# A state-space mixer and a mixture of experts on one core: the mixer's first half rebuilt by channel

## The chip, the cores and the metric

The kernel runs on one core of one Trainium2 chip. The metric is device time in microseconds (us), the median of several executions. The engines are TensorE (PE; its weight loads are listed as PEld), VectorE (DVE), ScalarE (ACT), GpSimd (POOL) and SyncE (SP), which issues most transfers; ScalarE and GpSimd can issue transfers too.

## The reference, cut to what matters

The input is 8 batches of 512 steps with 128 features, all in float32.

```python
xz = einsum('bld,ed->bel', hidden, W_in); x, z = split(xz)     # 256 channels each
x = silu(causal_conv(x, conv_w, 4 taps per channel) + conv_b)
dtA = exp(log_dt)[:, None] * (-exp(log_A_real) + 1j * A_imag)  # 256 channels x 8 states
Ct = (C_re + 1j * C_im) * (exp(dtA) - 1) / A
k = 2 * real(einsum('hn,hnl->hl', Ct, exp(dtA[:, :, None] * arange(512))))
y = causal_convolution(x, k) + x * D                           # along the 512 steps
y = y * silu(z)
x1 = layernorm(hidden + einsum('bhl,dh->bld', y, W_out))
e = argmax(x1 @ gate_w.T + gate_b + expert_bias)               # one of 8 experts per token
out = layernorm(x1 + relu(x1 @ w1[e] + b1[e]) @ w2[e] + b2[e])
```

## The kernel before, in words

The 4096 tokens are cut into 32 chunks of 128 steps (4 per batch). The long convolution is computed in chunks: inside a chunk by a Toeplitz matrix of the first 128 kernel values, across chunks through the 8 complex states of each channel, for up to three chunks back. The 256 channels form 32 groups of 8.

**Projection (0 to 80 us).** `project` (line 1292) takes 16 steps of two chunks. For each chunk it multiplies the input by four weight matrices `Wx`, one per tap, each already scaled by that tap's weight per channel (line 873), so the four-tap convolution happens inside TensorE's accumulation; `project_gates` (line 1275) adds the product for z. VectorE adds the bias and stores x with the channel in the free dimension (`bias`, line 881), ScalarE stores z (`keep_z`, line 643). Beside this the two engines build the tables: `Ctab`, the powers of the states at steps 0 to 128, as an exponential times a sine with amplitude and phase (arctangent, square root), and `Btab` with `decay`, the same powers counted backwards for three lags, from rows that are sent to DRAM and broadcast. Line 1337 sums the states into kernel rows, which are stored to DRAM (line 414).

**Groups (80 to 130 us).** For each of 32 groups SP loads 512 KB of Toeplitz matrices from DRAM (`load_toeplitz`, line 424, a ring of 8). GpSimd forms the group's state table (`group_tables`, line 515). TensorE multiplies chunks by Toeplitz matrices (`convolve`, line 1370), sums states over three lags (`sum_states`, line 1357), transposes the first product back and adds the states' part (`finish`, lines 1380 and 1384). VectorE masks the states (`states`, line 1044) and multiplies the output by the gates (`output`, line 1057). ScalarE copies and applies Silu in between (lines 713 to 738).

**Quads (130 to 175 us).** Eight quads of four chunks, one batch each. TensorE transposes the gated output (`transpose_gated`, line 1418), ScalarE copies it (line 761), TensorE projects it with the output weights, the residual and the gate logits in one accumulation (lines 1433 and 1435). ScalarE sums squares (line 772), VectorE takes the reciprocal (line 1085), chooses the expert, normalizes (line 1122) and, with counts from TensorE (lines 1449 and 1451), finds each token's row. GpSimd then dispatches the rows: `dispatch` (line 568) sends 128 rows at a time to DRAM by an indirect transfer, each behind a small fill (`apart`, line 558). In the first 52 us SP has written empty rows over the whole buffer of slots (line 409, four transfers of 1.8 to 2.3 MB).

**Blocks (from 173 us).** 39 blocks of 128 rows, each for one expert. SP loads a block's rows (line 450, a ring of 12) and the expert's first weights (line 371, a ring of 4). TensorE transposes and multiplies (lines 1469, 1477, 1487), VectorE adds and normalizes, GpSimd stores each block by an indirect transfer (`store`, line 576), the first 24 behind a small fill. A slot of the row ring is loaded again only when the block twelve before it is stored.

The order on every engine is written out by hand. GpSimd's queue holds the group tables, then the constants of the counting, then all dispatches, then all stores. SP's holds the loads in the order of use.

## Time and profile before

| | us |
|---|---|
| device time, median of 3 runs | 269.08 (268.27 to 269.29) |
| span of the profiled execution, first to last instruction | 263.8 |
| the runs' median over that span | 5.3 |
| TensorE busy | 239.2 (91%) |
| ScalarE busy | 187.1 (71%) |
| VectorE busy | 177.0 (67%) |
| GpSimd busy | 139.8 (53%) |
| moved by DMA | 52.06 MB, 197 GB/s on the average |

The profiled execution's device time is known only through its span; the median less the span, 5.3 us, is what lies around it. Busy times are those of the whole span; the stages differ much. Columns of the groups below are named where they first occur.

### The profile page before, as it was taken

How to read it: one execution, taken by the hardware profiler on the slowest of the kernel's cores; microseconds unless marked ns; L12 is line 12 of the kernel's file. 1: busy time of each engine (PE TensorE's matmuls, PEld its weight loads, DVE VectorE, ACT ScalarE, POOL GpSimd, SP SyncE). 2: the span in 40 equal slices, each digit the busy share in tenths (PEclk: the TensorE clock that was granted, in tenths of full speed). 3: DMA queues.
4: the chain of work that ended last, by engine and by line, in shares of the span. 5: the costliest groups of instructions: out<-in, count | busy, mean ns of one | idle time of the engine just before them, and what ended most of it. 6: DMA issues, size and time to landing. Idle time of an engine off the chain costs nothing.

```text
span 263.8 us, 8892 instructions
## 1 busy us (share of the span) xinstructions
PE 239.2 (91%) x2763; PEld 215.1 (82%) x2764; DVE 177.0 (67%) x552; ACT 187.1 (71%) x528; POOL 139.8 (53%) x208
## 2 busy tenths in 40 slices
PE   8999979999999899999979999359989999999970
PEld 4888768888887678888869999349979999899960
DVE  1889995997218657777724878842877676566672
ACT  2999999856998778888655665207667777667740
POOL 6000000400009989999624687878746656657545
PEclk9999999999999999999999999759999999999995
DMA  7697884600399999999293221647865676677600
GB/s 232 180 313 288 346 334 150 244 0 0 105 310 332 310 279 296 308 320 302 66 361 120 93 93 41 212 92 191 220 179 172 200 210 164 203 195 208 189 34 6
DMA packets 54267, 52.06 MB, mean 197 GB/s; under 512 B 4415, under 2 KB 42817, under 8 KB 54114
## 3 DMA queue, kind: packets, MB, share of 16 engines
q1 hardware_dynamic: 51506, 46.65, 59.2%
q0 software_dynamic: 2304, 4.34, 4.6%
q10 hardware_dynamic: 432, 0.79, 0.8%
q8 instruction: 11, 0.18, 0.3%
q14 instruction: 14, 0.11, 0.1%
HBM read 38.14 MB, written 14.07 MB: 198 GB/s over the span
## 4 chain that ended last, share of the span: by engine, by line
PE 59%; DVE 10%; ACT 10%; POOL 9%; issue 6%; DMA 5%; SPq 1%; DVEq 0%; ACTq 0%; POOLq 0%
PE banks L1292 13%; PE banks L1477 9%; PE banks L1487 8%; PE banks L1370 7%; POOL dispatched_rows L568 5%; ACT BR L672 5%; PE banks L1380 5%; PE banks L1384 4%; PE banks L1275 3%; PE banks L1357 3%; PE banks L1435 2%; DMA X<-dispatched_rows 2%; POOL RE L558 1%; DMA out<-X 1%; POOL out L576 1%
## 5 line engine op out<-in xcount | busy, mean ns | idle before, releaser
L515 POOL TENSOR_TENSOR Wx<-BR,RE 128x384 f32 (+1 forms) x32 | 47.9, 1548 | 27.9 <-PE banks L1292 26.6
L1292 PE MATMUL banks<-Wx,XT 128*128 128x256 f32 x256 | 59.9, 380 | 1.7 <-ACT Z L643 1.7
L809 ACT ACTIVATE Z<-banks,BR 128x128 f32<-128x128 f32 x156 | 44.6, 368 | 18.4 <-PE banks L1477 18.3
L1292 PEld LDWEIGHTS banks<-Wx,XT 128*128 128x128 f32 x256 | 48.4, 190 | 9.0 <-issue 2.2
L576 POOL DMA_INDIRECT out<-X x39 | 38.4, 986 | 27.8 <-DVE X L1233 15.3
L1477 PE MATMUL banks<-Z 128*128 128x128 f32 x312 | 42.7, 281 | 0.4 <-ACT Z L798 0.2
L1487 PE MATMUL banks<-BR,Z 128*128 x312 | 41.1, 276 | 1.2 <-DVE X L1216 1.2
L1477 PEld LDWEIGHTS banks<-Z 128*128 128x128 f32 x312 | 39.0, 196 | 1.0 <-issue 0.5
L1487 PEld LDWEIGHTS banks<-BR,Z 128*128 128x128 f32 x312 | 37.8, 192 | 1.5 <-issue 1.5
L568 POOL DMA_INDIRECT dispatched_rows<-TR,CR x32 | 31.0, 970 | 9.3 <-POOL RE L558 9.3
L1057 DVE TENSOR_TENSOR X<-banks,Z 128x256 f32 (+1 forms) x32 | 20.4, 636 | 9.1 <-PE banks L1384 9.1
L521 POOL MEMSET RE<- 128x128 f32 x1 | 0.2, 205 | 44.0 <-DVE CR L989 44.0
L1370 PE MATMUL banks<-TR,RE 128*32 128x128 f32 x512 | 21.3, 279 | 1.4 <-issue 1.2
L1216 DVE TENSOR_TENSOR X<-banks,X 128x128 f32<-128x128 f32 x39 | 11.3, 289 | 14.9 <-PE banks L1487 13.4
L881 DVE TENSOR_TENSOR X<-banks,cbias 128x512 f32<-128x512 f32 x15 | 15.3, 1062 | 8.5 <-PE banks L1275 8.4
L1435 PE MATMUL banks<-Wx,RE 128*128 128x136 f32 x128 | 20.1, 279 | 0.0
L1370 PEld LDWEIGHTS banks<-TR,RE 128*32 128x32 f32 x512 | 12.3, 109 | 9.4 <-ACT RE L713 5.8
L798 ACT ACTIVATE Z<-banks 128x128 f32<-128x128 f32 x39 | 11.3, 289 | 10.8 <-PE banks L1469 10.3
L1275 PE MATMUL banks<-Win,XT 128*128 128x256 f32 x64 | 18.5, 381 | 0.0
L772 ACT ACTIVATE RE<-banks 128x128 f32<-128x128 f32 x32 | 8.9, 278 | 13.2 <-PE banks L1435 8.8
L558 POOL MEMSET RE<- 128x128 f32 x56 | 12.7, 226 | 9.1 <-DVE CR L1141 7.9
L1044 DVE SCALAR_TENSOR_TENSOR Win<-banks,RE,mask 128x192 f32<-128x192 f32 x32 | 13.4, 418 | 6.1 <-PE banks L1357 4.3
(220 smaller groups left out, 469.6 us busy)
## 6 DMA issues: line engine op xcount, KB each, us to landing
TR<-kernel_rows SPq DMA_DIRECT2D x32, 512.0 KB, 6.5
Z<-w SPq DMA_DIRECT2D x39, 256.0 KB, 3.1
dispatched_rows<-TR SPq DMA_DIRECT2D x3, 2310.0 KB, 8.8
X<-dispatched_rows SPq DMA_DIRECT2D x39, 66.0 KB, 2.1
XT<-hidden_t SPq DMA_DIRECT2D x10, 256.0 KB, 3.1
RE<-decay_and_turns SPq DMA_DIRECT2D x2, 1024.0 KB, 7.4
BR<-w SPq DMA_DIRECT2D x1, 2048.0 KB, 8.2
dispatched_rows<-TR SPq DMA_DIRECT2D x1, 1848.0 KB, 7.8
```

Source lines behind the costliest of these rows:

```text
L515: nc.gpsimd.tensor_tensor(BC[:, k, 0:LAGS, :].rearrange("p m (s r n) -> p (m s) r n", s=STRIPS, r=2), Btab[:, :, :, :, :, one].rearrange(" ...
L558: nc.gpsimd.memset(pause[:, 0:columns], 0.0).then_inc(s_pause, 1)
L568: pool.indirect_dma_start(slots_dram, bass.IndirectOffsetOnAxis(pos[:, batch, k:k + 1], 0), X1[:, batch, k, :], None).then_inc(s_sc[batch] ...
L576: pool.indirect_dma_start(out_rows, bass.IndirectOffsetOnAxis(XS[:, n % ROWS_RING, TOKEN_COL:TOKEN_COL + 1].bitcast(U32), 0), F[:, slot, : ...
L809: last = nc.scalar.activation(HT[:, j, c * P:c * P + P], bank[UP_BANKS[j]][:, c * P:c * P + P], ACT.Relu, bias=B1[:, bass.ds(experts[j] * ...
L1057: tt(group, bank[4 + k][:, 0:GH * TILES].rearrange("p (h t) -> p h t", h=GH), gates, ALU.mult).then_inc(s_yc, 1)
L1275: return mm(bank[Z_BANKS[k]][:, j * CHAN:(j + 1) * CHAN], XT[:, slot, at:at + CHUNK], Win[:, CHAN:], start=True, stop=True)
L1292: last = mm(bank[X_BANKS[k]][:, j * CHAN:(j + 1) * CHAN], XT[:, slot, at:at + CHUNK], Wx[:, tap, :], start=(tap == 0), stop=(tap == TAPS - 1))
L1370: last = mm(yt[part:part + TILES, at:at + P], xg[:, h, :], Tring[:, k, h, :], start=True, stop=True)
L1435: last = mm(projected(slot, k), GT[:, slot, k, j * P:j * P + P], Wo[:, j, :], start=False, stop=(j == 1))
L1477: last = mm(bank[UP_BANKS[m % 4]][:, c * P:c * P + P], WS[:, stage, c * P:c * P + P], XsT[:, m % DEEP, :], start=True, stop=True)
L1487: last = mm(bank[DOWN_BANKS[m % 2]][:, 0:P], HT[:, m % DEEP, c * P:c * P + P], W2[:, e, c * DM:(c + 1) * DM].rearrange("p e d -> p (e d)") ...
```

## The change

The mixer is rebuilt with the channel in the partitions. `project_x` and `project_gates` are now one multiplication each over 512 steps for 128 channels (16 units of x and 16 of gates: 2 channel halves by 8 batches). The taps are added outside TensorE: ScalarE takes the last tap and the bias (`last_tap`), VectorE adds the other three from PSUM (`add_taps`). `turn_x` transposes each unit back, `keep_x` stores it with Silu, `keep_z` stores the gates with Silu.

The tables are rebuilt too. One table of powers `Etab` replaces `Ctab`, `Btab` and `decay`. Sines and cosines are taken at 28 angles only (16 fine, 8 coarse, 3 lags, one half step); GpSimd expands them to 128 steps by products of coarse and fine powers (`expand_half`, two halves of 16 groups), after it has formed the states' weights. `products`, the scratch of that expansion, lies in the upper half of X, and ScalarE waits for the second half of the powers (`s_e1`) before it stores unit 8 there. TensorE transposes the powers (`turn_powers`), sums local states per four groups (`sum_local`), turns them over three lags by matrices `Rot` that GpSimd forms (`turning`, `turn_states`), and adds them to the output by two multiplications of 64 rows each (`add_states`).

The kernel rows are summed and stored in two halves; SP loads five groups' Toeplitz matrices behind the first half and the others behind the second; the ring has 5 places instead of 8. Each group's output is copied (`keep_y`) into a ring of 4 and returned by one GpSimd transfer (`send_y`) of 128 KB into Y, where the channel lies in the partitions, four partitions per group. After the last transfer Y is multiplied by the gates per quad, quads 1, 3 and 5 by GpSimd, the others by VectorE (`gate`). TensorE's transpositions in the quads and ScalarE's copies of them go. All eight batches of the input stay in SBUF. The rows that no token takes are no longer emptied over the whole buffer: SP writes 128 empty rows behind each expert's last row, eight small transfers ahead of blocks 8 to 11.

The core of the diff:

```diff
+        def expand(engine, out, part, by_coarse, by_fine):
+            count = part.stop - part.start
+            shape = [P, count, COARSE, FINE]
+            return engine.tensor_tensor(
+                out.rearrange("p g (b a) -> p g b a", b=COARSE), by_coarse[:, part, :].unsqueeze(3).to_broadcast(shape),
+                by_fine[:, part, 0:FINE].unsqueeze(2).to_broadcast(shape), ALU.mult)
...
+            store_rows(0)
+            for g in range(T_SLOTS):
+                load_toeplitz(g)
+            store_rows(1)
+            for g in range(T_SLOTS, GROUPS):
+                load_toeplitz(g)
...
+            def expand_half(part, ready):
+                expand(nc.gpsimd, Etab[:, part, :], part, first_coarse, cosine)
+                done(expand(nc.gpsimd, products[:, part, :], part, second_coarse, sine))
+                tt(Etab[:, part, :], Etab[:, part, :], products[:, part, :], ALU.add).then_inc(ready, 1)
+
+            def send_y(g):
+                pool.wait_ge(s_yt, g + 1)
+                home = bass.AP(Y[:, :, :, :].tensor, g * 2 * TOKENS, [[GROUPS * 2 * TOKENS, 4], [2 * P, TILES], [1, 2 * P]])
+                pool.dma_start(home, YT[:, g % Y_RING, :]).then_inc(s_yd[g % Y_RING], 16)
+
+            pool.wait_ge(s_far, 1)
+            expand_half(slice(0, HALF), s_e0)
+            turning(slice(0, HALF))
+            expand_half(slice(HALF, GROUPS), s_e1)
...
+            for n in POOL_QUADS:
+                gate(nc.gpsimd, n).then_inc(s_gp, 1)
             nc.gpsimd.memset(OH[:, :, :, 4], 0.0)
             nc.gpsimd.memset(carry, 1.0).then_inc(s_oc, 1)
...
+            act.wait_ge(s_e1, 1)
+            keep_x(8)
+            last_tap(10)
+            for n in range(TURNS):
+                keep_y(4 * n)
+                if n + 1 < TURNS:
+                    keep_local(n + 1)
+                if n == 0:
+                    keep_rows(1)
+                    keep_powers(4)
...
+            def add_taps(u):
+                j = u // BATCH
+                dve.wait_ge(s_x3, u + 1)
+                for back in range(1, TAPS):
+                    if back > 1:
+                        dve.wait_ge(s_xk, u * LAGS + back - 1)
+                    stt(xc[:, u % 2, back:], bank[u % 2][:, 0:SEQ - back], channel[:, j, TAPS - 1 - back:TAPS - back],
+                        xc[:, u % 2, back:], ALU.mult, ALU.add).then_inc(s_xk, 1)
...
+            def add_states(g):
+                halves = output_banks(g)
+                pe.wait_ge(s_v, g + 1)
+                for j in range(2):
+                    rows = slice(j * 64, (j + 1) * 64)
+                    last = mm(halves[j][:, 0:P], V[rows, g % V_RING, :, :].rearrange("p h t -> p (h t)"), Etab[rows, g, :],
+                              start=False, stop=True)
+                last.then_inc(s_y, 1)
```

## Rows read from the trace of the kernel before

**Rows 1.** Busy time by stage: stretch, length, busy us (instructions), clock, DMA share, GB/s.

```profile
0.00:80.00 80.00, 77.02 (x394) 64.97 (x395) 58.01 (x111) 67.42 (x111) 8.40 (x37) 1.00 0.62 210
80.00:130.00 50.00, 48.53 (x1414) 39.66 (x1414) 34.83 (x66) 41.11 (x113) 47.50 (x34) 1.00 1.00 285
130.00:175.40 45.40, 36.04 (x294) 34.74 (x293) 30.35 (x143) 22.41 (x90) 28.64 (x57) 0.93 0.43 143
175.40:264.00 88.60, 77.64 (x663) 75.77 (x663) 53.80 (x234) 56.16 (x215) 55.24 (x82) 0.94 0.59 165
```

**Rows 2.** The chain of waits: start us, us, what.

```profile
36.37 0.43 PE banks L1275 x2
...
64.86 1.96 PE banks L1337 x64
...
81.90 0.57 PE banks L1370 x16
...
142.88 0.88 PE banks L1418 x8
...
148.76 0.96 POOL dispatched_rows L568
```

**Rows 3.** GpSimd in order of time: start us, us, engine, line, operation.

```profile
141.19 0.20 POOL L558 MEMSET RE<- 128x128 f32 x1 [7.10 <-DVE CR L1141]
...
188.43 0.96 POOL L568 DMA_INDIRECT dispatched_rows<-TR,CR  x1 [0.28 <-POOL RE L558]
...
190.42 1.00 POOL L576 DMA_INDIRECT out<-X  x1 [0.81 <-POOL RE L558]
...
261.07 0.98 POOL L576 DMA_INDIRECT out<-X  x1 [0.30 <-issue]
```

**Rows 4.** ScalarE in order of time, the start.

```profile
3.89 1.28 ACT L619 ACT_TABLE_LOAD   x1 [3.74 <-DMA RE<-states]
...
5.32 0.21 ACT L620 ACTIVATE RE<-RE 128x32 f32<-128x32 f32 x1
```

**Rows 5.** Groups of instructions on VectorE: busy us, mean ns of one, idle before.

```profile
L1122 DVE TENSOR_TENSOR TR<-banks,rs 128x512 f32<-128x512 f32 x8 | 5.3, 665 | 0.0
...
L983 DVE TENSOR_TENSOR BR<-BR 128x2064 f32<-128x2064 f32 x2 | 4.6, 2310 | 0.1
```

**Rows 6.** Groups of instructions on ScalarE.

```profile
L662 ACT ACTIVATE RE<-RE,tau 128x2048 f32<-128x2048 f32 x3 | 5.9, 1997 | 0.0
```

**Rows 7.** Groups of instructions on GpSimd.

```profile
L515 POOL TENSOR_TENSOR Wx<-BR,RE 128x384 f32 x30 | 44.9, 1549 | 1.3 <-PE banks L1357 1.2
...
L499 POOL MEMSET TR<- 128x1024 f32 x1 | 1.0, 952 | 0.0
...
L497 POOL TENSOR_TENSOR mask<-mask 128x8 f32<-128x8 f32 x1 | 0.2, 200 | 0.1
```

**Rows 8.** TensorE in order of time, one group and the next one's start.

```profile
126.58 0.64 PE L1370 MATMUL banks<-TR,RE 128*32 128x128 f32 x16
...
128.04 0.65 PE L1370 MATMUL banks<-TR,RE 128*32 128x128 f32 x16
```

**Rows 9.** Two stretches as in the first group; transfers: count, KB, us from issue to landing.

```profile
110.00:120.00 10.00, 10.00 (x308) 8.23 (x306) 7.26 (x14) 8.33 (x25) 10.00 (x8) 1.00 1.10 319
134.00:138.00 4.00, 3.16 (x29) 2.97 (x27) 0.42 (x3) 2.36 (x11) 0.08 (x1) 1.00 0.97 411
...
Z<-w SPq DMA_DIRECT2D x39, 256.0 KB, 3.1
...
out<-X POOLq DMA_INDIRECT x39, 3.1
...
dispatched_rows<-TR,CR POOLq DMA_INDIRECT x32, 2.4
kernel_rows<-TR SPq DMA_DIRECT2D x1, 256.0 KB, 2.1
```

**Rows 10.** VectorE in order of time, the first reciprocal of the quads.

```profile
137.44 0.18 DVE L1085 RECIPROCAL rs<-sd 128x4 f32<-128x4 f32 x1 [4.39 <-ACT sd L781]
```

More of the change, by code:

```diff
@@ new lines, in build, with angles @@
+        Etab = CR[:, 0:GROUPS * CHUNK].rearrange("p (g i) -> p g i", g=GROUPS)
+        products = x_flat[:, TOKENS:].rearrange("p (g i) -> p g i", g=GROUPS)
+        def angles(at):
+            return y_flat[:, at * GROUPS * ANGLES:(at + 1) * GROUPS * ANGLES].rearrange("p (g a) -> p g a", g=GROUPS)
+        fall, sine, cosine = angles(0), angles(1), angles(2)
+        coarse_home = y_flat[:, 3 * GROUPS * ANGLES:]
+        coarse_part, first_coarse, second_coarse = [
+            coarse_home[:, at * GROUPS * COARSE:(at + 1) * GROUPS * COARSE].rearrange("p (g b) -> p g b", g=GROUPS)
+            for at in range(3)]
@@ L194, in build @@
         cnt = late(400, 6 * KINDS).rearrange("p (i e) -> p i e", e=KINDS)
+        ends = late(344, EXPERTS, I32)
+        last_used = late(352, EXPERTS)
+        behind = late(360, EXPERTS)
         erow = EN[:, 2192:2200]
@@ new lines, in _ @@
+            for i in range(6):
+                keep_z(i)
+            keep_x(0)
+            last_tap(2)
+            keep_z(6)
+            keep_z(7)
+            keep_x(1)
+            last_tap(3)
+            for i in range(8, 12):
+                keep_z(i)
+            for u in range(2, 6):
+                keep_x(u)
+                last_tap(u + 2)
+                keep_z(u + 10)
+            keep_x(6)
+            last_tap(8)
+            keep_rows(0)
+            keep_powers(0)
+            keep_powers(1)
@@ new lines, in _ @@
+            dve.wait_ge(s_ch, 16)
+            add_taps(0)
+            dve.wait_ge(s_fell, 1)
+            for at, table in ((1, sine), (2, cosine)):
+                dve.wait_ge(s_sin, at)
+                tt(table[:, :, 0:DECAYED], table[:, :, 0:DECAYED], fall[:, :, 0:DECAYED], ALU.mult).then_inc(s_dwn, 1)
+            dve.wait_ge(s_dwn, 2)
+            far = slice(FINE, FINE + COARSE)
+            done(ts(coarse_part[:, :, :], sine[:, :, far], odd, None, ALU.mult))
+            done(stt(first_coarse[:, :, :], cosine[:, :, far], even, coarse_part[:, :, :], ALU.mult, ALU.add))
@@ L1063, in _ @@
             tt(gbias[:, 2, :], gbias[:, 0, :], gbias[:, 1, :], ALU.add).then_inc(s_ctr, 1)
[L1064 to L1071 removed]
+            for g in range(12, 20):
+                states(g)
             dve.wait_ge(s_gwp, 1)
[L1073 removed]
@@ L1185, in rows_of_blocks, with gate_quad @@
                 dve.wait_ge(s_first, 2 if at else 1)
-            dve.wait_ge(s_yc, GROUPS + LEAD)
+            def gate_quad(n):
+                if n < QUADS and n not in POOL_QUADS:
+                    gate(nc.vector, n).then_inc(s_gd, 1)
+            for k in range(Y_RING):
+                dve.wait_ge(s_yd[k], GROUPS // Y_RING * 16)
+            dve.wait_ge(s_z, UNITS)
+            gate_quad(0)
+            gate_quad(2)
             dve.wait_ge(s_cconst, 2)
@@ new lines, in convolve @@
+            def convolve(g):
+                halves = output_banks(g)
+                pe.wait_ge(s_t[g % T_SLOTS], (g // T_SLOTS + 1) * 16)
+                wait_past(pe, s_yt, g - 1)
+                for h in range(GH):
+                    part = h % 4 * TILES
+                    last = mm(halves[h // 4][part:part + TILES, 0:P], X[:, g * GH + h, :], Tring[:, g % T_SLOTS, h, :],
+                              start=True, stop=False)
+                last.then_inc(s_tm, 1)
+            def add_states(g):
+                halves = output_banks(g)
+                pe.wait_ge(s_v, g + 1)
[4 more added lines that the diff above has]
+                last.then_inc(s_y, 1)
@@ L1311, in _, with group @@
+            def group(g):
+                convolve(g)
+                add_states(g)
             pe.wait_ge(s_warm, 1)
             for j in range(WARMING):
[L1313 to L1318 removed]
@@ new lines, in _ @@
+            pe.wait_ge(s_win, 16)
+            project_x(0)
+            project_x(1)
+            for i in range(6):
+                project_gates(i)
+            pe.wait_ge(s_const, 2)
+            pe.wait_ge(s_z, 1)
+            turn_x(0)
+            project_x(2)
+            project_gates(6)
+            project_gates(7)
+            turn_x(1)
+            project_x(3)
+            for i in range(8, 12):
+                project_gates(i)
+            for u in range(2, 6):
+                turn_x(u)
+                project_x(u + 2)
+                project_gates(u + 10)
```

1179 lines of the change are left out of this document (525 added, 654 removed).

## The prediction, made before the change was run

> **What bounds the kernel now.** I read first the busy time by stage, because shares over the whole span mix stages that have different limits [rows 1]. The reader is to see four stages. Until 80 us TensorE is busy for 77 of 80 us: it projects the input and does the four-tap convolution by four multiplications with scaled weights. From 80 to 130 us the 32 groups pass, with TensorE busy for 48.5 of 50 us and the DMA engines full (share 1.00). From 130 to 175 us no engine is full on the average, and then 39 expert blocks follow. The chain of waits [rows 2] agrees for the first two stages (lines 1275 and 1337, and line 1370 after them) and then goes over to GpSimd: line 568, the dispatch of 128 rows at a time. The order of time on GpSimd [rows 3] shows why the end of the kernel hangs on that. The fill before the first dispatch starts at 141.19 us, the 32nd dispatch runs at 188.43 (32 at 1.46 us apart, with a gap of 1 us), the first store of an output block follows at 190.42, and the last store is issued at 261.07. Each block from number 12 on needs the slot of the block stored twelve before it. So from 141.2 us on the rest is one line of GpSimd work, and the end lies 263.8 - 141.2 = 122.6 us behind the first dispatch. TensorE has slack there (77.6 us of 88.6 in the block stage [rows 1]).
>
> So the question for this change is: when does the first dispatch start? All that it rebuilds lies before that point; behind it only the eight small fills behind the experts and their waits on SP are new, and they stand at block 8, where TensorE waits for GpSimd later anyway (cost 0; if that cover is gone, about 2 us for one late weight load, whose 256 KB take 3.1 us to land [rows 9]).
>
> **Part 1: the powers.** The new chain runs through all engines, then ends on GpSimd. The state parameters are there at 3.8 us; the first table load (1.28 us) is now taken ahead of them, so the two exponentials that ended at 5.5 us [rows 4] end at about 4.4. VectorE then forms four tables of 896 elements. At 2310 ns for 2064 elements [rows 5] one costs 1.0 us, and with two small operations and one cheaper pass the angles are ready at 4.4 + 5.5 = 9.9 us. ScalarE loads the sine table (1.28) and does two passes of 896 elements at 1997 ns for 2048 [rows 6], 0.9 each: 13.0. VectorE does the first unit's taps beside this. Its two products with the decay (1.0 each) and four small coarse tables (0.4 each) end at 16.7 us. GpSimd's small products, some sixteen of 0.2 to 0.3 us (an 8-element one takes 200 ns [rows 7]) in six dependent steps, and seven of 96 to 256 elements, take 6 to 8 us from 15 us on. GpSimd can begin the powers at about 23 us (22 to 25).
>
> Now the dear term. Each half of the powers is three products or sums over 2048 elements, and between the halves stands a turning matrix of 1536 elements: 6 x 2048 + 1536 = 13,824 elements in line on GpSimd. The trace has no such operation. Its bounds are a fill at 952 ns for 1024 elements (0.93 ns each) and the group-table product at 1549 ns for 384 (4.03 ns each), whose two inputs are read in steps of 32 elements [rows 7]. A fill has one stream; the product here reads two contiguous ones and writes one. If the reads take turns and the write lies beside them that is 1.86 ns, if all three take turns 2.8. I take 2.3, near the fill because nothing here is strided. A 2048-element operation is then 4.7 to 4.8 us, the whole line 32 us (bounds 13 and 56), and the second half is ready at 23 + 32.4 = 55.4 us. The Trainium skill (GPSIMD Engine Reference, section 3.1) gives 4497 ns for exactly such an addition over 2048 elements, as an estimate here; by it the second half would be ready some 1.5 us earlier.
>
> Why the second half, and not the first, decides: ScalarE waits for it before it stores x unit 8 (the product's scratch lies in that half of X), and everything behind that, the copy of group 0's output included, stands in ScalarE's queue. On SP the loads of groups 5 and on stand behind the second half of the kernel rows, and that behind the same powers. TensorE and VectorE are not later: the sixteen 512-column projections and sixteen gates cost 0.86 us each (two lots of 256 columns at 0.43 [rows 2]), and the taps cost VectorE three passes at about 0.7 us (665 ns for 512 elements out of PSUM [rows 5]), 2.2 to 2.4 us a unit, so that unit 8 is through at about 37 us, the moment at which the first half of the powers is ready (38). Group 0 can start at 38 + 1.0 (rows summed) + 0.7 (copied) + 2.1 (stored [rows 9]) + some 3.5 for its load = 45 us instead of 80; then, until 55, the kernel does little but wait for GpSimd.
>
> **Part 2: the groups.** After 55.4 us three turns of four groups are mixed with what is left. On TensorE that is half the kernel rows 1.0 (half of 1.96), four transpositions of powers and seven of x at 0.45 (eight single ones take 0.88 [rows 2]), five projections at 0.86, five lots of state sums at about 1.2, eleven groups of 0.57 (sixteen instructions of line 1370 [rows 2]) plus about 0.45 for the two 64-row halves: 28 us, and 3 us of round trips to ScalarE, 31 in all. The other 20 groups: TensorE needs 0.57 + 0.45 + 0.45, about the 1.46 us that one group takes now from one line 1370 to the next [rows 8]. Each also loads 512 KB. At 319 GB/s, the rate of a full stretch [rows 9], that is 1.64 us, and the returned output (128 KB) adds 0.39, so 2.03 a group; GpSimd's constants for the counting, which now stand between its 12th and 13th transfer (some fifteen fills and counts, about 4 us by the small operations of [rows 7]), are covered by the ring of four outputs, 8 us. Five loads are ahead, 15 x 2.03 = 30 us. The last group is done at 55.4 + 31 + 30 = 116.4 us, against 130 before [rows 1]. That gain of 14 us is what is left of the 25 to 30 that the earlier start promised.
>
> **Part 3: from the last group to the first dispatch.** Now 130 to 141.2, 11 us: TensorE's transpositions and projection lie between. New: copy 0.4 with hops 0.3, and the last transfer. A transfer issued by GpSimd lands 2.4 to 3.1 us after its issue [rows 9]; I take 3.1, and all is there at 120.2. Then three of the eight gate products run on GpSimd one after another, 1024 elements at 2.3 ns = 2.4 us, together 7.1 (bounds 2.9 and 12.4), and only behind them stand the fills that VectorE waits for before it chooses any expert. VectorE's own gate products (1024 elements, 1.2 us) run at the same time; whether they hold GpSimd up, no row shows: between 0 and 2.4 us, I take 1.2. The Trainium skill (SBUF — State Buffer, Who interferes with whom) says that a VectorE operation with two SBUF inputs and a GpSimd operation that reads SBUF exclude one another; no run here shows it, and by it this term would be 2.4 us. So 128.5; fills and VectorE's constants 1.1; its third gate product 1.2, placed ahead of the first choice; then from reciprocal to the dispatch's fill 141.19 - 137.44 = 3.75 us as now [rows 3, 10]. First dispatch: 134.6 us. The eight transpositions per quad and their copies go, but the gates' wait covers them: TensorE has projected quad 0 long before.
>
> **Sum.** 134.6 - 141.2 = -6.6 us on a span of 263.8. The profiled execution's span lies 5.3 us below the median of the runs, 269.08, which I take as the constant around it: 262.5 us.
>
> **Rivals.**
> (a) GpSimd multiplies at the rate of its strided product, 4.03 ns. The line of powers takes 56 us, not 32, and the gates 5 more: 262.5 + 24 + 5 = 291 us, slower. For it: it is the only large product on this engine in the trace. Against: that one strides, and its 1549 ns hold its start too. It decides from 2.8 ns on, where 13,824 elements have eaten the 6.6 us. The price is set by the stretch between 23 us and the second half's signal.
> (b) The returned outputs bound the groups. Each writes 128 KB into four partitions only, thirty-two apart. The full rate of the trace is 411 GB/s over 128 partitions [rows 9], 3.2 for each; if a partition takes no more, one transfer needs 10 us, four can be under way, and a group takes about (10.2 + 1.7) / 4 = 3.0 us. 15 x 3.0 = 45, +15, and the last lands 7 us later: +22. If neighbours' rate can be used it costs nothing. Half way: +11, 273.5 us, slower. The Trainium skill (SBUF — State Buffer, Door 1) has such partitions share two ports of about 27 GB/s each; by that estimate a transfer takes 2.4 us and the loss is about 8 us, 270.5. No run here shows a transfer into so few partitions.
> (c) GpSimd's reads alone set its rate (1.86 ns, 26 us for the line), its gates meet no resistance, and the three mixed turns lose nothing in round trips: -6 - 2.5 - 3, 251 us.
>
> **How the numbers follow.** Forecast 0.46 (own range 256 to 268), (a) 0.12, (b) 0.22, (c) 0.20. The predicted time is 262.5. The range reaches from 248, which holds most of (c), to 282, which holds most of (b) and leaves (a) out. A measurement can tell 0.5%, 1.35 us, from no change. Faster: (c) 0.20, the forecast but for its upper edge 0.41, a rest of (b) 0.02. Same 0.10: 0.04 of the forecast and 0.06 of (b). Slower: (a) 0.12, (b) 0.14, the forecast's edge 0.01.
>
> **What would show it.** GpSimd's products of 2048 elements near 4.7 us, the second powers' signal near 55 us with TensorE idle for some 6 us before it; the last group near 116; the three GpSimd gates in line after the last transfer; the first dispatch near 135 and an end 122 us behind it. The prediction is wrong if the groups don't wait for the powers, if a group takes over 2.3 us after the third turn, or if the end is no longer tied to the first dispatch.

## The result, and the profile after

The changed kernel takes 325.5 us (median of four runs, 323.9 to 327.4) against 269.2 before: ratio 1.213 [1.206, 1.221]. The forecast was 262.5 (248 to 282), so both the sign and the range were wrong. The profiled execution took 324.6 us with a span of 322.9, against 263.8 before. The ratios compare fast executions alone, and of the kernels below e9 and e14 were profiled in slow ones (276.2 and 271.5 us against medians of 272.6 and 267.5), so their stages read some 4 us late.

First the busy time by stage, with the columns of [rows 1] (stretch, length, busy us and instructions of PE, PEld, DVE, ACT, POOL, then clock, DMA share, GB/s):

```profile
0.00:48.50 48.50, 39.34 (x324) 20.92 (x325) 33.19 (x54) 31.10 (x53) 44.51 (x60) 0.96 0.37 111
48.50:84.00 35.50, 28.65 (x635) 18.82 (x635) 15.91 (x33) 16.66 (x33) 10.19 (x13) 0.90 0.95 166
84.00:120.00 36.00, 20.06 (x457) 14.18 (x457) 1.67 (x9) 4.39 (x12) 8.16 (x25) 0.63 1.17 165
120.00:164.00 44.00, 23.88 (x492) 16.12 (x484) 1.94 (x9) 4.89 (x13) 8.77 (x14) 0.66 0.86 154
164.00:192.00 28.00, 8.59 (x37) 8.00 (x36) 9.21 (x22) 3.64 (x12) 12.89 (x16) 0.56 0.29 101
192.00:323.00 131.00, 106.30 (x854) 103.68 (x852) 81.28 (x358) 68.83 (x279) 82.27 (x126) 0.90 0.47 136
```

The row to stop at is the third. The DMA engines are as busy as at the full rate before (share 1.17; 1.10 in [rows 9]; it adds up the times of packets, which can overlap, so it can pass 1), but they move 165 GB/s where they moved 319. A busy DMA engine is not a moving one: here it waits. TensorE is busy for barely more than half of the stretch, at a granted clock of 0.63 (partly at 1.2 GHz, the lower level); the loads it waits for are late. The page's list of transfers (KB each, median us from issue to landing) says which:

```profile
TR<-kernel_rows SPq DMA_DIRECT2D x32, 512.0 KB, 13.4
Y<-EN POOLq DMA_DIRECT2D x32, 128.0 KB, 9.8
```

A returned output lands after 9.8 us, where the forecast took 3.1 from [rows 9], and a Toeplitz load after 13.4. In the kernel before it was 6.5:

```profile
TR<-kernel_rows SPq DMA_DIRECT2D x32, 512.0 KB, 6.5
```

The chain of waits of the changed kernel (start us, us, what) from the mixed turns to the gates; "issue" is time in which the engine waits for nothing that the profile shows:

```profile
66.47 4.08 issue
...
83.92 4.79 issue
...
90.58 71.64 DMA TR<-kernel_rows x5
...
165.56 10.46 DMA Y<-EN
...
176.27 8.98 POOL Y L348 x3
```

For 71.6 us the end hangs on Toeplitz loads; then on the last returned output, 10.5 us; then on GpSimd's three gate products. GpSimd in order of time, against [rows 3] and [rows 7]:

```profile
21.95 3.67 POOL L342 TENSOR_TENSOR CR<-Y 128x2048 f32<-128x2048 f32 x1
...
43.99 4.54 POOL L570 TENSOR_TENSOR CR<-CR,X 128x2048 f32<-128x2048 f32 x1
...
191.74 0.20 POOL L617 MEMSET ET<- 128x128 f32 x1 [3.06 <-DVE CR L1047]
...
242.01 0.98 POOL L627 DMA_INDIRECT dispatched_rows<-TR,CR  x1 [0.28 <-POOL ET L617]
...
320.19 0.98 POOL L635 DMA_INDIRECT out<-Z  x1 [0.31 <-issue]
```

The powers are ready at 48.5 us, seven sooner than forecast. The first dispatch's fill stands at 191.7 (forecast 134.6), the end 131.2 us behind it (forecast 122.6).

### The profile page after: what moved, and what is told of

Read it like the earlier page. It is cut to its first block, busy times and chain, and to the rows that moved or that the text cites. A ratio compares the mean times of both kernels' runs of the same rounds, so it can differ in the third digit from the quotient of the medians.

```text
span 322.9 us, 8229 instructions
## 1 busy us (share of the span) xinstructions
PE 226.8 (70%) x2787; PEld 181.7 (56%) x2788; DVE 143.2 (44%) x484; ACT 129.5 (40%) x402; POOL 166.8 (52%) x253
## 4 chain that ended last, share of the span: by engine, by line
PE 34%; DMA 30%; POOL 15%; DVE 9%; issue 6%; ACT 3%; SPq 2%; ACTq 0%; DVEq 0%; POOLq 0%
DMA TR<-kernel_rows 22%; PE banks L1434 11%; PE banks L1444 9%; DMA Y<-EN 3%; POOL CR L570 3%; POOL Y L348 3%; PE banks L1268 3%; POOL CR L342 2%; POOL X L342 2%; PE banks L1196 2%; PE banks L1277 2%; DMA XT<-hidden_t 2%; PE banks L1211 2%; PE banks L1426 2%; DMA Z<-dispatched_rows 1%
## 5 line engine op out<-in xcount | busy, mean ns | idle before, releaser
L575 POOL DMA_DIRECT2D Y<-EN x32 | 22.4, 699 | 89.8 <-ACT EN L723 81.8
L635 POOL DMA_INDIRECT out<-Z x39 | 38.6, 988 | 28.3 <-DVE Z L1152 12.7
L852 ACT ACTIVATE Z<-banks,CR 128x128 f32<-128x128 f32 x156 | 44.8, 369 | 20.7 <-PE banks L1434 20.5
L1268 PE MATMUL banks<-TR,X 128*32 128x128 f32 x512 | 28.1, 352 | 28.7 <-DMA TR<-kernel_rows 27.3
L723 ACT ACTIVATE EN<-banks 128x256 f32<-128x256 f32 x32 | 12.3, 384 | 74.1 <-PE banks L1277 63.3
L1444 PE MATMUL banks<-X,Z 128*128 x312 | 41.9, 279 | 0.0
L902 DVE SCALAR_TENSOR_TENSOR xc<-banks,channel,xc 128x511 f32<-128x511 f32 (+2 forms) x48 | 35.6, 748 | 11.2 <-ACT xc L686 10.0
L1444 PEld LDWEIGHTS banks<-X,Z 128*128 128x128 f32 x312 | 38.7, 196 | 0.1
L1396 PE MATMUL banks<-Wox,Y 128*128 128x136 f32 x128 | 23.9, 317 | 12.1 <-DVE Y L348 12.1
L1396 PEld LDWEIGHTS banks<-Wox,Y 128*128 128x128 f32 x128 | 20.9, 226 | 12.5 <-DVE Y L348 12.5
L1277 PE MATMUL banks<-CR,EN 64*128 64x128 f32 x128 | 21.3, 415 | 4.8 <-issue 4.8
## 6 DMA issues: line engine op xcount, KB each, us to landing
TR<-kernel_rows SPq DMA_DIRECT2D x32, 512.0 KB, 13.4
```

What stands on the lines that cost most here:

```text
L575: pool.dma_start(home, YT[:, g % Y_RING, :]).then_inc(s_yd[g % Y_RING], 16)
L635: pool.indirect_dma_start(out_rows, bass.IndirectOffsetOnAxis(XS[:, n % ROWS_RING, TOKEN_COL:TOKEN_COL + 1].bitcast(U32), 0), F[:, slot, : ...
L852: last = nc.scalar.activation(HT[:, j, c * P:c * P + P], bank[UP_BANKS[j]][:, c * P:c * P + P], ACT.Relu, bias=B1[:, bass.ds(experts[j] * ...
L902: stt(xc[:, u % 2, back:], bank[u % 2][:, 0:SEQ - back], channel[:, j, TAPS - 1 - back:TAPS - back], xc[:, u % 2, back:], ALU.mult, ALU.ad ...
L1268: last = mm(halves[h // 4][part:part + TILES, 0:P], X[:, g * GH + h, :], Tring[:, g % T_SLOTS, h, :], start=True, stop=False)
L1277: last = mm(halves[j][:, 0:P], V[rows, g % V_RING, :, :].rearrange("p h t -> p (h t)"), Etab[rows, g, :], start=False, stop=True)
```

## The experiments

The stages below are times in the span, us, from each profiled execution: the last group's sums, the start of the gates, the first dispatch's transfer (0.7 us behind its fill), the end.

| kernel | last group | gates start | first dispatch | end | time |
|---|---|---|---|---|---|
| changed kernel | 164.1 | 176.2 | 192.4 | 322.9 | 325.5 |
| e1 wide | 125.5 | 133.7 | 150.0 | 280.5 | 282.2 |
| e2 ScalarE's queue | 170.7 | 182.8 | 199.0 | 325.8 | 327.5 |
| e3 four transfers | 184.9 | 198.0 | 214.1 | 343.1 | 344.9 |
| e4 four ports | 135.2 | 146.6 | 162.8 | 291.6 | 293.4 |
| e12 eight slots, narrow | 163.7 | 176.4 | 192.7 | 323.0 | 324.8 |
| e5 gates | 168.7 | 181.4 | 193.5 | 323.6 | 325.4 |
| e6 waits moved | 168.3 | 175.2 | 191.4 | 316.5 | 318.3 |
| e7 halves, all | 141.1 | 145.6 | 157.0 | 282.5 | 284.3 |
| e8 four ports, all | 134.2 | 140.1 | 152.2 | 276.3 | 278.1 |
| e9 scratch tensor, all | 128.8 | 135.2 | 147.5 | 274.5 | 272.6 |
| e10 thin | 122.6 | 130.1 | 145.0 | 275.3 | 277.0 |
| e11 eight slots, wide | 125.5 | 131.9 | 144.2 | 269.2 | 271.2 |
| e13 fewer matmuls | 142.4 | 148.8 | 160.9 | 287.3 | 289.1 |
| e14 clock and fills | 129.1 | 135.9 | 147.0 | 269.7 | 267.5 |
| e15 read-back ahead | 125.6 | 133.6 | 144.2 | 266.5 | 268.9 |

Times of the changed kernel, e9, e11, e14 and e15 are medians of several executions, the others single ones. The group loop itself varies: e5 and e6 leave it as it is in the changed kernel, and their last groups came 4.6 and 4.2 us later. Differences of this size in the column of the last group decide nothing by themselves.

### What makes the transfers late: e1 to e4 and e12

**e1**

```diff
-home = bass.AP(Y.tensor, g * 2 * TOKENS, [[GROUPS * 2 * TOKENS, 4], [2 * P, TILES], [1, 2 * P]])
+home = y_flat[:, g * 2 * P:(g + 1) * 2 * P]        # 128 partitions
```

> The group's output goes out on the same queue, by the same single GpSimd transfer of 128 KB, but each partition of YT into 256 columns of the same partition of Y: 128 destination partitions in place of four (Y then holds another layout, so the output is not the reference's). In the changed kernel the 32 transfers took 9.8 us (median) from issue to landing, a Toeplitz load 13.4 us, and the last group was done at 164.1 us; the time was 325.5 us. Theory A (four destination partitions take the data too slowly and hold up the engines that also carry the Toeplitz rows): transfers land in about 3 us, Toeplitz loads in about 6.5 us as before the change, last group at 110 to 120 us, end at 270 to 280 us. Theory B (a transfer with four rows of descriptors is carried by four of the 16 DMA engines only): the same here. Theory C (GpSimd's queue itself is slow): no change, 320 to 328 us. Theory D (the ring of five slots in place of eight holds the loads back): no change, 320 to 328 us.

**e2** (the same `home`, issued in `keep_y`)

```diff
-pool.dma_start(home, YT[:, g % Y_RING, :])
+act.dma_start(home, YT[:, g % Y_RING, :])
```

> The same transfer to the same four partitions, issued by ScalarE right after it has copied the group out, in place of GpSimd. Theory C (GpSimd's queue is slow): transfers land in about 3 us, last group at 110 to 120 us, end at 270 to 280 us. Theory A (four destination partitions): no change, transfers at 9 to 13 us, last group at 160 to 170 us. Theory B (four engines only): no change, or worse if ScalarE's queue takes the same four engines each time: last group at 165 to 190 us.

**e3**

```diff
+for h in range(4):
+    home = bass.AP(Y.tensor, (h * GROUPS + g) * 2 * TOKENS, [[GROUPS * 2 * TOKENS, 1], [2 * P, TILES], [1, 2 * P]])
+    act.dma_start(home, YT[h * TILES:(h + 1) * TILES, g % Y_RING, :])
```

> Again ScalarE's queue and the same four destination partitions, but four transfers a group, each of 32 rows of 1 KB into one partition. Theory B (the four-row shape limits a transfer to four engines): a transfer with 32 rows spreads over all engines, Toeplitz loads no longer wait for four slow engines; last group at 110 to 130 us, end at 270 to 290 us. Theory A (destination partitions): the partitions are the same, no change: last group at 160 to 175 us, end at 320 to 335 us. Theory C as in the run from ScalarE with one transfer: last group at 110 to 120 us.

**e4**

```diff
+def home_of(g):
+    return 16 * (0, 4, 1, 5, 2, 6, 3, 7)[g % 8] + g // 8
-home = bass.AP(Y.tensor, g * 2 * TOKENS, [[GROUPS * 2 * TOKENS, 4], ...
+home = bass.AP(Y.tensor, home_of(g) * 2 * TOKENS, [[4 * 2 * TOKENS, 4], ...
```

> GpSimd's single transfer as in the changed kernel, four destination partitions, but four partitions 4 apart inside one block of 16 (z's channels and the output weights are permuted to match), the block changing from group to group, in place of partitions 32 apart. Theory A, if it is the partitions' ways into the memory (the Trainium skill, SBUF - State Buffer, section Door 1, has partitions 32 apart share a port): twice as many ports, so transfers at 4 to 6 us, last group at 120 to 135 us, end at 280 to 295 us. If each single partition is what limits: no change. Theory B (four engines): no change, last group at 160 to 170 us. Theories C and D: no change.

The stretch 84 to 120 us of each, as the third row above, and the landing times where the page gives them. e1:

```profile
84.00:120.00 36.00, 27.94 (x857) 19.96 (x857) 3.61 (x18) 7.84 (x21) 11.61 (x35) 0.88 0.95 289
```
```profile
TR<-kernel_rows SPq DMA_DIRECT2D x32, 512.0 KB, 5.5
Y<-EN POOLq DMA_DIRECT2D x32, 128.0 KB, 4.5
```

e2:

```profile
84.00:120.00 36.00, 20.57 (x442) 14.37 (x446) 1.67 (x9) 4.11 (x11) 2.06 (x16) 0.57 0.64 164
```

e3:

```profile
84.00:120.00 36.00, 22.30 (x528) 15.91 (x524) 7.39 (x19) 7.66 (x18) 2.06 (x16) 0.78 1.07 162
```

e4:

```profile
84.00:120.00 36.00, 27.50 (x719) 19.62 (x718) 2.86 (x14) 7.03 (x19) 12.48 (x33) 0.76 1.00 239
```
```profile
TR<-kernel_rows SPq DMA_DIRECT2D x32, 512.0 KB, 7.5
Y<-EN POOLq DMA_DIRECT2D x32, 128.0 KB, 7.0
```

The same bytes on the same queue into 128 partitions: 289 GB/s, the last group 38.6 us sooner (125.5, which is still 5.5 behind what A expected; the rest is taken up further down). So C (the queue) falls. e2, another queue into the same four partitions, gains nothing either; its last group, at 170.7 us, lies in the range of B (four engines) and 0.7 past that of A.

B is not settled by e1, because the shape of the transfer changed with the destination. In the packet records of each run's first returned output, at most 6 of its packets are under way at a time in the changed kernel, 5 in e4, and 16 in e1. As the main cause B falls with e3 and e4. In e3, up to 13 packets of a group's output are under way at a time, and with the same destination it is slower than any of the theories allowed (last group at 184.9); from e2 to e3 the engines' share goes from 0.64 to 1.07 at the same 162 to 164 GB/s. What is left is the destination, and e4 says what of it: still four partitions and few packets at a time, but 4 apart, in a block that changes from group to group, and 28.9 of the 38.6 us are gained (239 GB/s). Whether the wider step inside a transfer or the change of block between transfers does it, no run separates; and the last 9.7 us, between e4 and e1, may belong to B or to the partitions.

The packet records agree: a 4 KB packet of a returned output took 403 ns on the average in the changed kernel, 227 in e4 and 162 in e1; a 512-byte packet of the Toeplitz rows 44.9, 32.6 and 28.5 ns (28.6 before the change). So beside the narrow writes the loads to all other partitions slowed too. That the same engines carry both is the likely way; the records don't name the engine of a packet. e2 is an exception that stays open: its Toeplitz packets took only 33.2 ns, and yet the loads landed after 15.2 us.

The Trainium skill (SBUF — State Buffer, Door 1: The DMA port swizzle) has partitions g and g + 32 share a port, so that four partitions 32 apart reach two ports and four partitions 4 apart reach four; the order of e4 and the changed kernel agrees. Its rate of a port priced the loss at 8 us in rival (b), where e1 gains 38.6: that price left out the other loads beside the narrow writes.

**e12** gave the changed kernel eight slots for Toeplitz rows (as e11 below) and nothing else.

> The changed kernel, four narrow destination partitions as they are, with the same eight slots and nothing else. Theory A (the narrow destination holds up the DMA engines themselves): more loads in flight only wait longer, last group at 158 to 168 us, time 318 to 328 us. Theory D (the ring of five is the larger part of the loss): last group at 120 to 140 us, time 280 to 300 us.

```profile
84.00:120.00 36.00, 16.18 (x419) 11.85 (x421) 1.67 (x9) 3.73 (x10) 7.47 (x24) 0.64 1.19 146
```

With the narrow destination more slots for loads change nothing (324.8 us, last group at 163.7): D falls there.

### Behind the last group: e5 and e6

**e5**

```diff
-POOL_QUADS = (1, 3, 5)
+POOL_QUADS = ()                       # VectorE gates all eight, quad 1 ahead of quad 2
```

> The changed kernel with all eight quads gated by VectorE, none by GpSimd. In the changed kernel GpSimd's three gates took 9.0 us in line, VectorE's two beside them 4.5 us, and from the start of the gates to the first dispatch it took about 16 us. Theory E (GpSimd's gates hold the dispatch, as the forecast had it): VectorE's gates take 1.2 us each, GpSimd comes to its dispatches 7 to 9 us sooner after the gates' start, and the time falls from 325.5 to 316 to 319 us. Rival (the projection, scale and choice behind the gates set the first dispatch anyway): the first dispatch comes at most 2 us sooner, time 323 to 327 us. The group loop is untouched: last group at about 164 us in both.

From the gates' start to the first dispatch it took 12.2 us in place of 16.2: 4 us, half of what theory E asked and twice what its rival allowed. The time did not move, because in this execution the group loop took 4.6 us longer (last group at 168.7); so the 4 us are read from the stage alone. VectorE in the changed kernel shows why the gates cost what they did (start us, us, ...):

```profile
176.24 4.51 DVE L348 TENSOR_TENSOR Y<-Y,Z 128x1024 f32<-128x1024 f32 x2 [34.07 <-DMA Y<-EN]
...
186.47 1.23 DVE L348 TENSOR_TENSOR Y<-Y,Z 128x1024 f32<-128x1024 f32 x1
```

Two of VectorE's products took 4.51 us beside GpSimd's (1.23 and 3.37), one alone 1.23; GpSimd's three took 3.40, 3.32 and 2.34, the last of them nearly alone.

**e6**

```diff
 sp.wait_ge(s_y, GROUPS)
+for k in range(Y_RING):
+    sp.wait_ge(s_yd[k], 16 * (GROUPS // Y_RING))     # ahead of B1, W2, B2
...
-if g == EARLY_BLOCKS - 4:                            # the eight fills
+if g == EARLY_BLOCKS:
...
-if s == 2: count(s)                                  # TensorE
 output_projection(s)
-if s != 2: count(s)
+count(s)
```

> The changed kernel with three waits moved and no work taken out: the loads of the experts' weights (B1, W2, B2) wait until the groups' outputs have landed; the eight fills behind the experts are issued behind the loads of blocks 8 to 11 in place of ahead of them; and quad 1 is projected ahead of the counting of quad 0. Theory F (the late landing, the fills ahead of block 8 and the gap in the dispatches are each a real term of the end): the last transfer lands 4 us after the last group in place of 11, TensorE's idle of 5.4 us ahead of block 8 goes, the gap of 3.3 us between dispatches 4 and 5 goes; time 309 to 316 us. Rival (something else is late right behind each, GpSimd's 32 dispatches and the loads of block 12 above all): 321 to 326 us.

From the last group to the gates: 7.0 us in place of 12.2. From the first dispatch to the end: 125.1 in place of 130.4. The time fell by 7.2 us to 318.3, with the last group 4.2 later; the expected 309 to 316 was for an equal loop and is missed by 2.3. Three waits moved at once, so how the 5.3 us behind the first dispatch divide is not shown. In the changed kernel SP and TensorE show the wait at block 8 (SP's fills, then TensorE's wait in brackets), and GpSimd the gap behind the fourth dispatch:

```profile
238.23 7.70 SPq L450 DMA_DIRECT2D dispatched_rows<-ET  x8
```
```profile
248.91 0.47 PE L1426 MATMUL banks<-ident,Z 128*128 128x128 f32 x1 [5.36 <-DMA Z<-dispatched_rows]
```
```profile
201.14 0.21 POOL L617 MEMSET ET<- 128x128 f32 x1 [3.27 <-DVE CR L1047]
```

### All together, and another way back: e7, e8, e9

e8 is e4 with the edits of e5 and e6; e7 the same with two transfers a group, of 64 KB each, to two lots of four partitions in different blocks.

> All of it together, with the output of each group sent in two GpSimd transfers of 64 KB, each to four partitions that lie 4 apart in one block of 16, the two blocks and those of the next group on different ports; gates on VectorE alone; weights, fills and projection moved as in the run before. Theory A (ports): packets of the returned outputs take about 165 ns as in the run with 128 destination partitions, last group at 113 to 120 us after the start of the span; with the terms E and F the time is 255 to 265 us, under the kernel before. If the number of partitions and not their ports counts, or the smaller rows of 512 B cost more: last group at 124 to 135 us, time 266 to 278 us.

> The same, but one transfer of 128 KB a group to four partitions 4 apart (four ports, as in the run e4). There the last group was done at 135 us and the time was 293.4 us. Terms E and F take off 7 to 9 and 6 to 14 us: 271 to 280 us. If halves on eight ports are no better than this, the two times are within 2 us of each other.

Halves are no better but worse (last group 141.1 against 134.2). Whether the rows of 512 bytes or the double number of transfers make it so, no run shows. It was expected that halves on more ports would do as well as 128 partitions: a miss, and the time lies above both of its ranges.

**e9**

```diff
-pool.dma_start(home, YT[:, g % Y_RING, :])
+pool.dma_start(sent[g, :, :], YT[:, g % Y_RING, :])           # DRAM, 128 partitions read
...
+for n in range(QUADS):
+    sp.dma_start(y_flat[:, n * 1024:(n + 1) * 1024], bass.AP(sent.tensor, n * 1024, [[8192, P], [1, 1024]]))
```

> A group's output leaves by one GpSimd transfer of 128 KB from 128 partitions into a scratch tensor in device memory (no narrow destination), and eight loads of 512 KB bring the quads back into Y on all 128 partitions once the last transfer has landed (z's channels and the output weights permuted to match). Gates on VectorE alone, fills and projection moved as before, weights loaded behind the quads. Theory A with terms E and F: groups run as in the run with 128 destination partitions (last group at 122 to 128 us of the span), the gates start 7 to 9 us behind it (a transfer's landing, then the first quad's load), the first dispatch 12 us behind that, the end 124 to 126 us on: span 265 to 273 us, time 267 to 275 us, about the kernel before (268 to 270 us). Rival (the detour through device memory costs the group loop as much as the narrow partitions did): last group beyond 134 us, time above 280 us.

272.6 us, ratio to the kernel before 1.022 [1.010, 1.033]: the destination is no longer narrow, the edits of e5 and e6 are in it as well, and together 53 of the 56 us are back. The detour takes 6.4 us from the last group to the gates, about as much as e8's direct way (5.9).

### What is left in the group loop: e10, e11, e13

**e10**

```diff
-home = y_flat[:, g * 2 * P:(g + 1) * 2 * P]
-pool.dma_start(home, YT[:, g % Y_RING, :])
+home = y_flat[:, g * 2 * P:g * 2 * P + 8]
+pool.dma_start(home, YT[:, g % Y_RING, 0:8])
```

> The run with 128 destination partitions, but each transfer carries 8 of the 256 columns (4 KB in place of 128 KB), and the gates square Z, so the outputs' return is left out and all else stays. It asks what the bytes of the return cost when the destination is wide (last group at 125.6 us there). If it is their share of the 16 engines (some 0.3 us a group for 20 groups): last group at 115 to 120 us, 6 to 10 us sooner. If the rest of the loop's delay against the forecast's 116.4 us lies elsewhere (ring of five, TensorE's clock): last group at 123 to 127 us.

**e11** (slots: five as before, a sixth in `Sel`, two more in `xc` and `Rot` from group 16 on)

```diff
+def slot_of(g):
+    return g % 6 if g < 16 else 6 + g % 2 if g < 18 else slot_of(g - 8)
```

> The run with the scratch tensor (e9, 272.6 us), with more slots for the Toeplitz rows: six from the start (the selectors' home serves once the kernel rows are summed), eight from group 16 on (the last taps' buffer and part of the turning matrices). With hardly any bytes returned (e10) the last group was still at 122.6 us and SyncE's loads waited 47.7 us for slots, so Theory D (the ring of five) is asked again, now with a wide destination. If the ring holds the loads back: the DMA engines' share behind 84 us rises from 0.8 to 1.0 or more, a group takes 2.0 to 2.1 us, last group at 115 to 120 us of the span, time 261 to 267 us, under the kernel before (269 us). If not (the bandwidth or TensorE's half clock sets the loop): last group at 124 to 129 us, time 270 to 274 us.

Neither the bytes nor the slots are the main cause of what is left. Without the bytes the last group came 2.9 us sooner than in e1 (122.6, just outside what either answer expected), with eight slots it stands at 125.5, as in e1 (e9, the same with five, 128.8). The chain of waits of e11 between 84 and 120 us names nothing in the gaps:

```profile
88.36 0.72 issue
...
92.87 1.61 issue
...
97.12 3.02 issue
...
108.68 3.10 issue
```

With the stretch 84 to 120 us of e11 this closes the account of TensorE: 27.54 busy and 8.45 standing still (the four above) are 35.99 of 36.0 us. So TensorE and its standstills set the loop there, at a granted clock of 0.81:

```profile
84.00:120.00 36.00, 27.54 (x816) 19.74 (x814) 3.24 (x17) 7.07 (x19) 10.96 (x34) 0.81 0.91 273
```

In the packet records the three long ones stand with 16 KB packets of the instruction queue, which took 0.9 us each at 92.0, 97.9 and 109.4 us. This is no accident of e11: between 76 and 123 us e1, e9, e10, e11, e14 and e15 have 28 standstills of over 0.9 us, and every one of them ends 1.2 to 1.7 us behind the end of such a packet (not every packet has a standstill). The page counts that queue's packets, for e11, for e13 and for the kernel before:

```profile
q8 instruction: 19, 0.31, 0.4%
```
```profile
q8 instruction: 13, 0.21, 0.3%
```
```profile
q8 instruction: 11, 0.18, 0.3%
```

The kernel before passed its 32 groups in a loop on TensorE, four rounds of eight groups, where the changed kernel has them written out. From 80 to 130 us the kernel before has 3 of these packets beside its 1414 matmuls [rows 1] and one standstill of 0.95 us; e11 has 9 packets.

**e13**

```diff
-for strip in range(STRIPS):            # sum_local: 4 a group
-    last = mm(bank[3][rows, ...], ET[:, g, rows], x_chunks[:, at:at + PAIR, :, 0:LAGS])
+last = mm(bank[3][:, ...], ET[:, g, :], x_chunks[:, at:at + PAIR, :, 0:LAGS])
...
-    for strip in range(STRIPS):        # turn_states: 12 a group
+    last = mm(out_s[:, :, lag:], Rot_flat[:, first:first + P], local[:, :, 0:LAGS - lag], ...)   # 3
```

> The run with eight slots (e11, last group at 125.5 us, time 271.2 us), with each turn's state matmuls issued as 16 large ones in place of 64 by 32-row strips (the sums over tokens and the turning both; all rows then use the first strip's channels, and the turning mixes strips, so the states are not the reference's). In e11 TensorE stood still for 2.1, 1.5, 3.0 and 3.1 us between 80 and 112 us, each time around one of the 16 KB packets of the instruction queue (at 80.4, 92.0, 97.9 and 109.4 us). Theory G (TensorE's code loading cannot keep up with so many short matmuls): fewer of these packets, standstills under 3 us in all between 80 and 125 us, last group at 114 to 119 us, time 261 to 267 us. Rival (a wait that the profile does not name, on the states or the rows): the standstills stay at 8 to 10 us, last group at 123 to 127 us, time 269 to 274 us.

```profile
84.00:120.00 36.00, 36.00 (x364) 29.17 (x367) 3.63 (x17) 7.15 (x19) 9.51 (x31) 0.68 0.93 278
```

The standstills are gone: TensorE is busy for 36.00 of 36 us, with 364 matmuls recorded in place of 816. By itself e13 does not prove the cause, since a TensorE that is slower would also cover any other wait. Together with the packets above, each standstill ending behind one, the runs speak for code loading and against an unnamed wait on states or rows. The time forecast with it failed by 22 us: the four strips had run side by side, and one turning of four groups now took 2.8 us (5.2 at the lower clock) where it took 1.0 in the changed kernel. The chains, first of the changed kernel, then of e13:

```profile
81.47 0.98 PE banks L1258 x83
```
```profile
86.06 2.78 PE banks L1281 x24
...
106.34 5.23 PE banks L1281 x24
```

What the loop would be with the old matmuls and no standstill, or with the new groups in a loop on TensorE, no run shows.

### In search of a version under the kernel before: e14, e15

**e14**

```diff
+for k in range(20):                                   # TensorE, behind the last group
+    mm(bank[0][:, 0:2 * P], ident[:, :], XT[:, 0, 0:2 * P], start=True, stop=True)
...
-if g == EARLY_BLOCKS:                                 # SP: all eight fills
+if g <= EARLY_BLOCKS - 4:                             # four ahead of blocks 4 to 7, four ahead of 8 to 11
```

> The run with eight slots (e11, 271.2 us), with 20 matmuls of no use on TensorE between the last group and the first projection, and the eight fills issued in two fours, ahead of the loads of blocks 4 to 7 and of blocks 8 to 11, in place of all behind block 11. In e11 TensorE's granted clock was 0.5 at 132 to 138 us, the projections of quad 0 took 0.91 us a pair in place of 0.46, and TensorE stood idle for 2.9 us at 201 us, with the fills issued at 194.7 and block 12's rows loaded from 202.1 us, though the ends were ready at 175.7 us. If clock and fills are both real terms: the first dispatch comes 10 us behind the gates' start in place of 12.3, the idle at 201 us goes, time 263 to 267 us, under the kernel before (268 to 269 us). If GpSimd's dispatches set the end anyway: 269 to 272 us.

TensorE at 132 to 138 us, first in e11, then in e14:

```profile
132.00:138.00 6.00, 4.80 (x21) 4.80 (x22) 5.85 (x9) 0.74 (x4) 0.00 (x0) 0.50 1.02 415
```
```profile
132.00:138.00 6.00, 6.00 (x30) 5.28 (x29) 2.06 (x2) 0.00 (x0) 1.97 (x11) 1.00 0.84 301
```

The clock stayed at its upper level, 2.4 GHz; the first dispatch came 11.0 us behind the gates' start (12.3), the end 122.7 behind it (125.0). Ratio to the kernel before: 0.998 [0.994, 1.002]. That is no difference, at the edge of what was expected.

**e15** reads 7/8 of quads 0 and 1 back behind the 28th group, and has 15 idle matmuls.

> The run before (e14, 267.5 us, 0.998 of the kernel before) with two changes behind the last groups: 7/8 of quads 0 and 1 are read back as soon as the first 28 groups' outputs have landed, so that only 16 partitions of each follow the last transfer, and 15 matmuls of no use in place of 20, since the 20 ran until 1.3 us past the first gate. In e14 the gates started 6.8 us behind the last group and the first dispatch came 11.0 us later. If the two are terms of the end: gates 5 to 6 us behind the last group, the first dispatch 9.5 to 10.5 us later, time 264.5 to 266.5 us, ratio to the kernel before 0.988 to 0.996. If the early read-back holds up the last Toeplitz loads by as much, or the loop's own spread hides it: 266.5 to 268.5 us.

1.003 [0.998, 1.008]: no gain. Its chain has the last transfer, issued beside the early read-back, at 4.90 us in place of 1.96 in e9; that the read-back holds it up is likely, not shown. The chains of e15 and then of e9:

```profile
126.33 4.90 DMA group_outputs<-EN
...
131.30 2.21 DMA Y<-group_outputs
```
```profile
129.52 1.96 DMA group_outputs<-EN
```

No version came under the kernel before.

## Why the prediction was wrong

The span is 65.7 us above the forecast's 257.2 (the first dispatch at 134.6, and 122.6 behind it): 47.7 to the last group, 9.4 from there to the first dispatch, 8.6 behind it. The 47.7 are 6.9 gained on the powers, 11.7 lost in the mixed turns and 42.8 in the 20 groups behind them.

- **The powers: the mechanism right, the size too large.** Products of 2048 elements took 3.67, sums 4.54 to 4.55 us, forecast 4.7 to 4.8; the second half was ready at 48.5, not 55.4. The whole line took 26.6 us, close to the 26 of rival (c). Rival (a) falls.
- **The mixed turns: too short, and hidden by luck.** Twelve groups were done at 91.2 us, in e1 at 84.0; forecast 86.4. This looks near only because the powers came early: from the powers on, the turns took 42.7 us, in e1 34.0, against 31. In the changed kernel two standstills of 4.08 and 4.79 us lie in them (the chain above); both end 1.3 to 1.5 us behind a packet of the instruction queue that took 1.5 and 1.6 us. The forecast had no such term.
- **The returned output: the step that failed.** It was put at "the returned output (128 KB) adds 0.39" a group (at 319 GB/s it would be 0.41) and a landing of 3.1, as if its destination were as wide as the others. It landed after 9.8 and beside it a Toeplitz load landed after 13.4; 20 groups took 72.8 us, not 30. A wide destination gives 38.6 of the 47.7 us back. This was rival (b), with its place right (four partitions, 32 apart) and its price too small: its upper bound, +22 us, counted the transfers' own time and not what they do to the loads beside them.
- **Five loads ahead, 15 x 2.03: failed too.** With a wide destination 20 groups still took 41.5 us (e1; 41.4 in e11). TensorE's 1.47 a group was taken from rows at full clock without standstills, of groups that ran in a loop. In e11 it stood still for 8 to 10 us, and ran part of the time at the lower clock. The standstills stand with its code loads (e11, e13).
- **The last landing: failed.** 12.2 us from the last group to the gates, forecast 3.8: the transfer lands behind the loads of B1, W2 and B2, issued in the same moment. Behind a wait it was 7.0 (e6).
- **GpSimd's gates: right.** 9.0 us forecast 8.3. The 1.2 put for VectorE's interference measured 2.0 (3.40 + 3.32 - 2 x 2.34). The Trainium skill (SBUF — State Buffer, Who interferes with whom), by which the term was 2.4, agrees. On VectorE all gates together bring the dispatch 4 us forward (e5).
- **The fills at block 8, "cost 0": failed.** SP spent 7.7 us on them, in line ahead of blocks 8 to 11, and TensorE stood for 5.4. A gap of 3.3 us in the dispatches came on top: quad 1's projection stood in TensorE's queue behind the counting of quad 0. Both moved, the end lies 125.1 us behind the first dispatch's transfer in place of 130.4 (e6). With the fills in two fours it is 122.7 (e14), 123.4 counted from the fill as the forecast's 122.6 is.
- **The constant around the span** is 1.7 us, not 5.3: the execution profiled before must have been nearer 265.5 than 269 us. This raised the forecast by 3.6 us.

## What to carry to other kernels

Before a transfer into few partitions is priced by its bytes, ask which partitions: with four others (e4), or with all 128 (e1, e9), most of the loss here was gone, for a narrow destination slowed all other loads too. A high DMA share beside a low rate in GB/s is one sign of it; e2 lost as much at a share of 0.64, so look at the times to landing as well. Many short matmuls written out one after another can cost TensorE code loads: look for standstills that nothing explains, and hold them against the instruction queue's packets. And a rate taken from rows of a loop need not hold for the same work written out.

## What the runs showed of the hardware that was not expected

- Four partitions 32 apart: 403 ns for a 4 KB packet. Four partitions 4 apart, in changing blocks: 227. 128 partitions: 162. Packets of other transfers, to all partitions, slowed from 28.5 to 44.9 ns.
- More packets at a time into the narrow destination made it worse: four transfers a group (e3) ended 17 us behind one (e2), at the same 162 to 164 GB/s from 84 to 120 us.
- TensorE stood still for 1.5 to 3.1 us around 16 KB code packets of 0.9 us, three times in the 36 us from 84 us on in e11, which has 64 short state matmuls a turn, and not once in e13, which has 16. In six runs all 28 such standstills end 1.2 to 1.7 us behind the end of a packet.
